# Step 2 of a round: VectorE shifts the scores of unit 3 ahead of the low part of the turned x

## The reference

```python
x = x + attention(layernorm(x), ctx, ctx)        # 16 heads of 16, softmax over 77 keys, w_q w_k w_v w_o with biases
logits = layernorm(x) @ router_w                 # 8 experts
probs = softmax(logits); top_w, top_i = top_k(probs, 2)
for e in range(8):
    h = silu(xn @ gate_w[e]) * (xn @ up_w[e])
    out = out + cw[:, e:e + 1] * (h @ down_w[e])
x = x + out
```

## Time and profile before

| what | us |
|---|---|
| timed runs | 911.65, 908.09, 916.79 |
| their median | 911.65 |
| the profiled execution, its own time | 910.35 |
| its span in the trace | 908.5 |

### The profile page before, as it was taken

How to read it: one execution, slowest core, us unless ns; L and a number is a source line. 1 busy time by engine, 2 the same in 40 slices (tenths; PEclk the granted TensorE clock), 3 DMA queues, 4 the chain that set the end, 5 groups by cost and what they waited for, 6 DMA issues and landing times.

```text
span 908.5 us, 32045 instructions
## 1 busy us (share of the span) xinstructions
PE 843.3 (93%) x11936; PEld 770.9 (85%) x11936; DVE 588.6 (65%) x1757; ACT 479.8 (53%) x900; POOL 342.4 (38%) x637
## 2 busy tenths in 40 slices
PE   4889899899999987799999999999999999999995
PEld 3677777777777776699999999999999999999995
DVE  6789788788888756566466457446646648544442
ACT  5777777788887774444354335324424435333331
POOL 4789566655666555241122221222222122222112
PEclk9999999999999989899999999999999999999999
DMA  6211322222222543495355228225525632223221
GB/s 211 88 46 45 95 76 66 80 79 68 84 82 66 110 147 119 93 201 132 50 99 122 29 55 174 36 39 108 118 30 99 135 60 36 35 29 32 35 35 18
DMA packets 109876, 74.04 MB, mean 81 GB/s; under 512 B 66444, under 2 KB 99802, under 8 KB 109818
## 3 DMA queue, kind: packets, MB, share of 16 engines
q1 hardware_dynamic: 83898, 36.09, 16.9%
q0 software_dynamic: 13536, 19.85, 12.3%
q10 hardware_dynamic: 12384, 17.35, 7.5%
HBM read 36.27 MB, written 26.80 MB: 69 GB/s over the span
## 4 chain that ended last, share of the span: by engine, by line
PE 75%; issue 5%; ACT 4%; DVE 4%; POOL 1%; DMA 1%; another core or an unknown queue 1%; ACTq 0%; SPq 0%; DVEq 0%; POOLq 0%
PE bank L630 16%; PE bank L632 16%; PE bank L631 16%; PE bank L825 6%; PE bank L827 6%; PE bank L826 6%; PE bank L699 3%; PE bank L706 3%; ACT probs L938 1%; ACT pt_hi L944 1%; DMA raw_tail<-expert_rows 1%; DVE xt_lo L1155 1%; PE bank L755 1%; ACT xt_hi L925 1%
## 5 line engine op out<-in xcount | busy, mean ns | idle before, releaser
L630 PE MATMUL bank<-xg,e_hi 128*128 128x128 f16 x2176 | 374.6, 220 | 5.2 <-issue 3.4
L632 PE MATMUL bank<-xg,e_lo 128*128 128x128 f16 x2176 | 374.6, 220 | 0.5 <-issue 0.5
L631 PE MATMUL bank<-xg,e_hi 128*128 128x128 f16 x2176 | 374.6, 220 | 0.0
L1702 POOL DMA_INDIRECT out<-y_sb,tok_row x67 | 108.4, 1618 | 425.8 <-DVE y_sb L1456 404.2
L630 PEld LDWEIGHTS bank<-xg,e_hi 128*128 128x128 f16 x2176 | 214.0, 98 | 7.2 <-issue 3.1
L631 PEld LDWEIGHTS bank<-xg,e_hi 128*128 128x128 f16 x2176 | 214.0, 98 | 2.8 <-issue 1.2
L632 PEld LDWEIGHTS bank<-xg,e_lo 128*128 128x128 f16 x2176 | 214.0, 98 | 0.0
L1008 ACT ACTIVATE g_act<-bank 128x512 f32<-128x512 f32 x136 | 81.2, 597 | 223.0 <-PE bank L632 207.1
L1461 DVE SCALAR_TENSOR_TENSOR h_full<-bank,g_act 128x512 f32<-128x512 f32 x136 | 94.0, 691 | 121.7 <-ACT g_act L1008 120.7
L825 PE MATMUL bank<-e_hi,h_hi 128*128 128x256 f16 x544 | 148.9, 274 | 4.5 <-DVE h_lo L1467 3.1
L827 PE MATMUL bank<-e_hi,h_lo 128*128 128x256 f16 x544 | 148.8, 274 | 0.9 <-issue 0.8
(11 more groups left out here) (193 smaller groups left out, 1685.8 us busy)
## 6 DMA issues: line engine op xcount, KB each, us to landing
e_stage<-in_gate_w ACTq DMA_DIRECT2D x24, 256.0 KB
e_stage<-in_up_w ACTq DMA_DIRECT2D x22, 256.0 KB
e_stage<-in_down_w ACTq DMA_DIRECT2D x20, 256.0 KB
expert_rows<-pads SPq DMA_DIRECT2D x8, 530.0 KB
xin<-in_x SPq DMA_DIRECT2D x16, 256.0 KB, 3.0
xres<-in_x SPq DMA_DIRECT2D x16, 256.0 KB
out<-x SPq DMA_DIRECT2D x16, 256.0 KB
k_diag<-k_parts SPq DMA_DIRECT2D x124, 9.6 KB
```

Source lines behind the costliest of these rows:

```text
L630: pe.matmul(dst, a_hi(c), b_hi(c), start=c == 0, stop=False)
L631: pe.matmul(dst, a_hi(c), b_lo(c), start=False, stop=False)
L632: mm = pe.matmul(dst, a_lo(c), b_hi(c), start=False, stop=ends and c == chunks - 1)
L1702: pool.indirect_dma_start(out, bass.IndirectOffsetOnAxis(tok_from[:], 0), y_from[:], None, compute_op=ALU.add).then_inc(added, 16)
```

## The change

One entry moves from the table of stages ahead of the shift to the table of stages behind it. In step 2 VectorE now issues maximum of unit 3, shift of unit 3, `low_x`, `low_att`; before it was maximum of unit 3, `low_x`, shift of unit 3, `low_att`.

```diff
-                inner = {2: [(a, low_x)],
-                         3: [(n, lambda j: sum_x(j, 0, xin, x_in, 16, x_summed)),
+                inner = {3: [(n, lambda j: sum_x(j, 0, xin, x_in, 16, x_summed)),
                              (r, lambda j: high_rows(j, rows_at(j)))]}
                 outer = {0: [(a, full_kv)],
                          1: [(c, lambda j: normalize(j, 1))],
-                         2: [(c, low_att)],
+                         2: [(a, low_x), (c, low_att)],
```

## The result

| kernel | median, us | range, us | runs |
|---|---|---|---|
| before | 911.9 | 908.09 to 918.71 | 20 |
| changed | 919.32 | 915.4 to 925.96 | 20 |

The ratio is 1.0078, with a 95% interval from 1.0059 to 1.0097: the change **costs 0.8%, some 7 us**. The forecast of 911.5 us was wrong, and the time lies beyond the range of 906 to 917.5. The sign was the slower rival's; its mechanism was not.

What follows compares the result with a forecast made beforehand. It took TensorE, busy 93% of the span, as the bound. The profiled 910.35 + 0.1 - 0 gave 910.45 us; the same sum on the median gave 911.75, stated as 911.5, range 906 to 917.5.

Steps and rivals of the forecast that it cites:

- slower rival: Step 2, VectorE: shift delays low_x, 0.39 us in 15 rounds, 917.5 us (7%); harder form, waiting for the transpose, 922.3 (2%).
- The shift goes first: Step 2, VectorE: shift of unit 3 runs about 258.85 to 259.33, inside idle time; low_x still starts at 260.74.
- a shift at step 2 that waits for line 699: Changed profile, VectorE: listed among the signs that would show the forecast wrong; no size given.
- The unknown: ScalarE's unexplained 0.90 us idle ahead of pt_hi: at most 8.1 us gained or lost over nine rounds, taken as zero.
- What comes earlier: ScalarE's exponential of unit 3 gains 0.35 us, VectorE's low_att 0.39 us; TensorE absorbs it, costed at nothing.
- No DMA moves: Whole change: the swap adds or removes no instruction and moves no DMA; no time was charged for it.
- Faster rival: Steps 2 to 4: the earlier exponential reaches TensorE, 0.35 us in each of 15 rounds, 5.3 us, time 906.4; 8%.
- Larger effects: Loop rounds: a phase shift lengthens or shortens later waits, up to 0.90 us a round; 3% in all.

Runs made afterwards that it cites:

- e12: Kernel before with all four scatters of a round apart (fourth behind split_kv of the next round, first ahead of the context work): 900.80 us, ratio 0.9909.
- e14: Changed kernel with all four scatters of a round apart: 901.09 us, ratio 0.9873.
- e16: Kernel before with all four scatters of a round apart, timed again: 902.33 us, ratio 0.9884.
- the ten traces: Ten rounds each of ten traces of kernels with scatters in pairs, among them before and changed, 100 rounds in all; compares the scatter's start, unit 3's last matmul and inv_sum.
- e2: Kernel before, old VectorE order, with the token_i update and its wait moved behind the first two scatters, so these start earlier: 934.56 us, ratio 1.0247.
- e3: Kernel before with each of the 64 indirect scatters replaced by three GpSimd copies, expert tiles reading padding rows: 888.91 us, ratio 0.9774.
- e17: Kernel before with each scatter made a plain DMA of all columns, issued by GpSimd at the same place into another tensor: 888.89 us, ratio 0.9767.
- e7: Kernel before with scatters moving 16 of 265 columns into another tensor: 921.32 us, ratio 0.9999, on the chip where before takes 919 us.

## Why the prediction was wrong

- *"The shift goes first"*, inside idle time, at no price: the price held, the picture did not. I took the record's end of `turn_probs` of unit 1, 257.82, as the time at which its waiters may go. They may go 1.8 us later. The shift waits 0.76 us for it and leaves 0.57 us ahead of `low_x`, not 1.5; a shift at step 2 that waits for line 699 was one of my own signs of being wrong. It was saved by what I named as the excluding reason: `xt_hi` stands behind the same update.
- *"The unknown"*: **the failed step.** I bounded a 0.90 us wait on "remote" and took zero because I saw "no way by which the swap reaches it". Its cause, the scatter pair at 256.69 and 258.02, could be read from GpSimd's rows of the same stretch: a wait on "remote" in ten rounds should have made me list what every other engine did in it. I never read GpSimd's order. In the round shown that wait is still there after the swap; the swap changed which other updates are held up.
- *"What comes earlier ... I cost all of it at nothing"*: **the other half of the failure.** The 0.35 us on ScalarE came as computed (exponential of unit 3 at 0.47 behind `low_probs`), and TensorE did absorb it. But I followed it to TensorE alone. It also passes through `x2n` and `high_rows` to GpSimd, whose scatter starts 0.36 us earlier, and there being earlier is a loss. The term taken as nothing was in fact 0.8 us a round in the near-median execution, 0.5 of it at the lower clock. "No DMA moves" was true of the order and false of the time.
- *Slower rival* (`low_x` pushed back): did not occur as a price. From 80 to 345 us `low_x` starts 0.03 us after the end of `xt_hi` in ten rounds of twelve, and 0.29 to 0.43 us after it in two; TensorE's waits for `xt_lo` are 3.3 us together before, 2.1 and 2.8 after.
- *Faster rival*: did not occur; the 0.35 us reached no one who could use it.
- *"Larger effects"*, at 3%: a loss in the rounds beyond any rival's mechanism is what happened, with the clock as a multiplier that I had not priced: three low stretches in ten rounds of a near-median execution, against none.

## What to carry to other kernels

Follow a step that becomes earlier along every engine, to each DMA that GpSimd issues, and ask what it will fall on there. Where several engines are released at one instant by an operation that ended 1 to 2 us before, look for an indirect DMA of GpSimd at that time. Keep such DMAs away from one another and from the matmul groups whose completion others wait for; here that gave 1%.

## What the runs showed of the hardware

- TensorE's semaphore updates come late while GpSimd issues an indirect DMA. Matmuls that end from about 0.5 us after its start are hit: by 0.3 to 0.8 us with one DMA alone (e12, e14, e16), by 0.6 to 1.3 us and up to 1.9 us with two back to back (the ten traces, e2). TensorE itself goes on working, and the updates of VectorE and ScalarE are on time. Three copies on GpSimd in its place don't do it (e3), nor do plain DMAs of 0.55 us (e17); the bytes don't matter (e7). By what path it happens, and what in the indirect form does it, no run tells.
- In this kernel that costs some 22 us of 911 (e3, e17), a third to a half of which comes back by spacing the scatters (8 to 12 us with all four apart).
- One of the chips runs the kernel before in 919 us, the others in 911. Its mean granted clock is 0.978 there and 0.982 to 0.984 on the others, which is 4 to 6 of the 8 us; why the clock differs is open.
